# Graph convolutions in blocks of 49 tiles instead of 56, with 25 gathered and 24 picked tiles in each

## The reference, cut to what matters

```python
def rgcn_conv(x, src, dst, edge_type, W, root, bias):      # called twice, W1 and W2
    x_src = x[src]
    for r in range(8):
        msg = msg + jnp.where((edge_type == r)[:, None], x_src @ W[r], 0)
    agg = segment_sum(msg * norm[:, None], dst, ...)
    return agg + x @ root + bias

def _nnconv(x, src, dst, edge_attr, ew, eb, rw, rb):       # called three times
    W = (edge_attr @ ew + eb).reshape(E, 16, 16)
    msg = jnp.einsum('ei,eio->eo', x[src], W)
    agg = segment_sum(msg, dst, ...)
    return agg + x @ rw + rb
```

## Time and profile before

| | |
|---|---|
| three runs, median (lowest to highest) | 14911.91 us (14904.42 to 14941.55) |
| the profiled execution | 14959.53 us, its span 14958.3 us |
| DVE, POOL, PE, ACT busy over the span | 75%, 62%, 55%, 32% |
| the five convolution passes together | some 6.1 ms of the span |

### The profile page before, as it was taken

How to read it: one execution, slowest core, us unless ns; L and a number is a source line. 1 busy time by engine, 2 the same in 40 slices (tenths; PEclk the granted TensorE clock), 3 DMA queues, 4 the chain that set the end, 5 groups by cost and what they waited for, 6 DMA issues and landing times. The chain is left out here.

```text
span 14958.3 us, 147756 instructions
## 1 busy us (share of the span) xinstructions
PE 8297.6 (55%) x41291; PEld 5702.8 (38%) x41291; DVE 11150.7 (75%) x19230; ACT 4791.5 (32%) x2765; POOL 9259.2 (62%) x6976
## 2 busy tenths in 40 slices
PE   1222222222220688588836566665668858885886
PEld 0111111111110566466623233333356646663664
DVE  6999999999998566466635455554559967995996
ACT  0111111111110466456621001010037746773774
POOL 6777777777752466556655555555337756774776
PEclk5555555555555899789967777787779989997998
DMA  2444444444441222122211111111123323332332
GB/s 83 156 154 153 153 153 156 157 154 153 153 157 40 84 63 67 53 61 67 65 42 36 37 37 34 38 36 37 27 69 114 111 79 100 113 111 67 114 111 73
DMA packets 629773, 1371.10 MB, mean 92 GB/s; under 512 B 262833, under 2 KB 403118, under 8 KB 554126
## 3 DMA queue, kind: packets, MB, share of 16 engines
q1 hardware_dynamic: 405534, 1076.25, 20.0%
q0 software_dynamic: 224112, 293.30, 8.8%
HBM read 656.16 MB, written 712.80 MB: 92 GB/s over the span
## 5 line engine op out<-in xcount | busy, mean ns | idle before, releaser
L536 POOL DMA_INDIRECT h<-in_x,idx x1568 | 3051.7, 1946 | 1206.2 <-DMA efT<-in_edge_attr_t 785.3
L550 PE MATMUL PS<-waug,efT 17*128 17x256 f32 x6272 | 1129.4, 679 | 3167.2 <-DVE e L587 2179.1
L1681 PE MATMUL PS<-hot,lhs 128*128 128x392 bf16 x9408 | 1855.5, 355 | 1228.4 <-issue 762.8
L1668 POOL DMA_INDIRECT myg<-node_table,mix x1568 | 1662.6, 1060 | 1323.1 <-DVE mmsg L1737 797.5
L550 PEld LDWEIGHTS PS<-waug,efT 17*128 17x128 f32 x6272 | 695.2, 313 | 3600.9 <-DVE e L587 2225.8
L1681 PEld LDWEIGHTS PS<-hot,lhs 128*128 128x128 bf16 x9408 | 954.6, 103 | 2129.6 <-issue 1111.2
L1305 PE MATMUL PS<-every_weight,dstf 112*128 112x144 f32 (+1 forms) x8960 | 1313.8, 291 | 493.9 <-DVE dstf L1405 409.0
L1305 PEld LDWEIGHTS PS<-every_weight,dstf 112*128 112x128 f32 x8960 | 1252.3, 197 | 666.4 <-DVE dstf L1405 466.6
L1752 DVE TENSOR_TENSOR lhs<-mkx,m 128x512 bf16<-128x512 bf16 x1176 | 429.5, 421 | 1439.2 <-remote 1092.3
L571 ACT ACTIVATE cf<-cf 128x256 f32<-128x256 f32 x196 | 81.7, 417 | 3843.9 <-DVE e L614 3843.9
L1283 POOL DMA_INDIRECT c0yg<-node_table,c0ix x672 | 859.0, 1278 | 591.7 <-DMA c0ix<-in_src 288.3
(11 more groups left out here) (393 smaller groups left out, 18785.4 us busy)
## 6 DMA issues: line engine op xcount, KB each, us to landing
softmax_maxima<-M SPq DMA_DIRECT2D x196, 1024.0 KB, 8.6
softmax_denominators<-ST SPq DMA_DIRECT2D x196, 1024.0 KB
softmax_numerators<-ST SPq DMA_DIRECT2D x196, 1024.0 KB
r0rb<-pick_b SPq DMA_DIRECT2D x56, 512.0 KB
r0ra<-pick_a SPq DMA_DIRECT2D x56, 512.0 KB
r1rb<-pick_b SPq DMA_DIRECT2D x56, 512.0 KB
r1ra<-pick_a SPq DMA_DIRECT2D x56, 512.0 KB
c0rb<-pick_b SPq DMA_DIRECT2D x56, 512.0 KB
```

Source lines behind the costliest of these rows:

```text
L536: PO.indirect_dma_start(h[b.k][:, q, :], None, io["x"], bass.IndirectOffsetOnAxis(ap=idx[b.k][:, q:q + 1], axis=0))\
L550: mm = PE.matmul(PS[0:CH, 4 * message + 2 * (n % 2) + r, 0:C2], efT[b.k][row:row + D + 1, n // 2, :], waug[row:row + D + 1, C2 * message:C ...
L1668: PO.indirect_dma_start(yg[b.k][:, q, :], None, table8, bass.IndirectOffsetOnAxis(ap=ix[b.k][:, q:q + 1], axis=0))\
L1681: mm = PE.matmul(PS[:, 6 + k, 0:A7 // 2], lhs[(G * b.k + q) % 2][:, r, part, :], hot[4 * ((G * b.k + q) % 2) + r][:, k * A7 // 2:(k + 1) * ...
```

## The change

The blocks become 49 tiles (`TBC`, `NBC = 49, 32`) with 25 gathered and 24 picked tiles (`NG`, `HG = 25, 6`), for all five passes. Slots by three take the place of slots by two in `hot_`, in the PSUM banks of the picked rows (3, 4, 5) and in `mx`; the two loads of 2048 index columns (`ra`, `rb2`) become three of 1024 columns, each with a semaphore of its own. DVE's list of a block is regrouped: five scalings of five tiles, and 11 halvings instead of 13 for c (5 instead of 6 for r); the final add of r, the carry and the scan stand behind the last group. Cut to its core:

```diff
-TBC, NBC = 56, 28
-NG, HG = 24, 8
+TBC, NBC = 49, 32
+NG, HG = 25, 6
...
-            NSC, NTR = (6, 13) if both else (0, 6)
+            NSC, NTR = (5, 11) if both else (0, 5)
...
-            hot_ = [sb(f"{name}hot{k}", [128, KT, 512], F32R, L) for k in TWO]
-            ra = [sb(f"{name}ra{k}", [128, 2048], I16, L) for k in TWO]
-            rb2 = [sb(f"{name}rb{k}", [128, 2048], I16, L) for k in TWO]
-            mx = [dstf[0:A9 * D, 512 * k:512 * k + 512] for k in TWO]
+            hot_ = [sb(f"{name}hot{k}", [128, KT, 512], F32R, L) for k in range(3)]
+            ra = [sb(f"{name}ra{k}", [128, 1024], I16, L) for k in range(3)]
+            rb2 = [sb(f"{name}rb{k}", [128, 1024], I16, L) for k in range(3)]
+            mx = [dstf[0:A9 * D, 512 * k:512 * k + 512] for k in range(3)]
...
                     if m0 == 0:
                         PE.wait_ge(*h_cv.at(groups(b, q + 1)))
-                        if due(m := groups(b, q - 1)):
+                        if due(m := groups(b, q - 2)):
                             PE.wait_ge(*h_mk.at(m))
                     for m in range(m0, m1):
-                        mm = PE.matmul(PS[0:A9 * D, 4 + q % 2, :], parts[:, m % 2, m // 2, :],
-                                       hot_[q % 2][:, m // 2, :], start=(m == 0), stop=(m == 2 * KT - 1))
+                        mm = PE.matmul(PS[0:A9 * D, 3 + q % 3, :], parts[:, m % 2, m // 2, :],
+                                       hot_[q % 3][:, m // 2, :], start=(m == 0), stop=(m == 2 * KT - 1))
...
                 def widen(b, q):
-                    if due(n := groups(b, q - 1)):
+                    if due(n := groups(b, q - 2)):
                         S.wait_ge(*h_g.at(n))
...
                 def mask(b, q):
-                    if due(n := groups(b, q - 1)):
+                    if due(n := groups(b, q - 2)):
                         V.wait_ge(*h_sel.at(n))
...
                 def scale_gathered(b, n):
-                    ts = slice(4 * n, 4 * n + 4)
+                    ts = slice(5 * n, 5 * n + 5)
...
-                    if b and not both:
-                        add_typed(b, 8)
-                        add_typed(b, 9)
+                    if b:
+                        if not both:
+                            add_typed(b, 6)
+                        carry_in(b)
+                        by_destination(b)
```

More of the change, by code:

```diff
@@ L1165, in program @@
         c_ix, c_co, c_st = pair("c_ix"), pair("c_co"), pair("c_st")
-        h_ra, h_rb = pair("h_ra"), pair("h_rb")
-        c_ix, c_co, c_st, h_ra, h_rb = ([Since(x) for x in two_] for two_ in (c_ix, c_co, c_st, h_ra, h_rb))
+        c_ix, c_co, c_st = ([Since(x) for x in two_] for two_ in (c_ix, c_co, c_st))
+        h_ra, h_rb = ([Since(sem(f"{n}{j}")) for j in range(3)] for n in ("h_ra", "h_rb"))
         c_sc, c_pr, c_al, c_tr, c_msg = (Since(sem(n)) for n in ("c_sc", "c_pr", "c_al", "c_tr", "c_msg"))
@@ L1210, in conv_sync, with rows, load_low, load_high @@
             def conv_sync():
[L1211 to L1215, removed]
+                def rows(b, j, from_):
+                    return from_[some(b, NG + 8 * j, 8), :].rearrange("(a t) c -> a (t c)", a=1).to_broadcast([128, 1024])
+                def load_low(b, j):
+                    if due(n := b.on(-1).count(3 * KT, KT * j + KT)):
                         SP.wait_ge(*h_oh.at(n))
                         SP.nop(nofuse=True)
-                    SP.dma_start(rb2[half][:, :], rows(b, half, pick_b)).then_inc(h_rb[half].sem, 16)
-                def load_high(b, half):
-                    if due(n := groups(b.on(-1), 4 * half + 4)):
+                    SP.dma_start(rb2[j][:, :], rows(b, j, pick_b)).then_inc(h_rb[j].sem, 16)
+                def load_high(b, j):
+                    if due(n := groups(b.on(-1), 2 * j + 2)):
                         SP.wait_ge(*h_mk.at(n))
                         SP.nop(nofuse=True)
-                    SP.dma_start(ra[half][:, :], rows(b, half, pick_a)).then_inc(h_ra[half].sem, 16)
+                    SP.dma_start(ra[j][:, :], rows(b, j, pick_a)).then_inc(h_ra[j].sem, 16)
                 def load_ix(b):
@@ L1246, in first @@
                 def first(b):
-                    for half in TWO:
-                        load_low(b, half)
-                        load_high(b, half)
+                    for j in range(3):
+                        load_low(b, j)
                     for k in TWO:
                         load_ix(b.on(k))
+                    for j in range(3):
+                        load_high(b, j)
+                    for k in TWO:
                         load_co(b.on(k))
-                    for half in TWO:
-                        load_low(b.on(1), half)
-                        load_high(b.on(1), half)
+                    for j in range(3):
+                        load_low(b.on(1), j)
+                        load_high(b.on(1), j)
                 def body(b):
@@ L1330, in widen @@
                 def widen(b, q):
-                    S.wait_ge(*h_oh.at(b.count(4 * KT, KT * (q // 2) + KT)))
-                    if due(n := groups(b, q - 1)):
+                    S.wait_ge(*h_oh.at(b.count(3 * KT, KT * (q // 2) + KT)))
+                    if due(n := groups(b, q - 2)):
                         S.wait_ge(*h_g.at(n))
                     at = 512 * (q % 2)
-                    S.activation(hot_[q % 2][:, :, :], hb[q // 2 % 2][:, :, at:at + 512], ACT.Copy).then_inc(h_cv.sem, 1)
+                    S.activation(hot_[q % 3][:, :, :], hb[(3 * b.k + q // 2) % 2][:, :, at:at + 512], ACT.Copy).then_inc(h_cv.sem, 1)
                 def copy_always(b, q):
@@ L1381, in one_hot @@
                 def one_hot(b, j, c):
-                    if j > 3:
-                        b, j = b.on(1), j - 4
+                    if j > 2:
+                        b, j = b.on(1), j - 3
                     if not b.exists():
@@ L1386, in one_hot @@
                     if c == 0:
-                        if j % 2 == 0:
-                            V.wait_ge(*h_rb[j // 2].at(b.count(16, 16)))
+                        V.wait_ge(*h_rb[j].at(b.count(16, 16)))
                         if due(n := groups(b, 2 * j - 2)):
                             V.wait_ge(*h_cv.at(n))
-                    V.tensor_scalar(hb[j % 2][:, c, :], rb2[j // 2][:, 1024 * (j % 2):1024 * (j % 2) + 1024], pick[:, c:c + 1], None,
-                                    ALU.is_equal).then_inc(h_oh.sem, 1)
+                    V.tensor_scalar(hb[(3 * b.k + j) % 2][:, c, :], rb2[j][:, :], pick[:, c:c + 1], None, ALU.is_equal)\
+                        .then_inc(h_oh.sem, 1)
                 def one_hots(nx, p, n):
```

73 lines of the change are left out of this document (34 added, 39 removed).

## The result

The changed kernel takes **15570.84 us** (15521.41 to 15594.16, 4 runs), the kernel before 14926.48 us beside it: ratio 1.0429, 95% interval 1.0395 to 1.0462. The sign of the forecast was right, its size (15150, up to 15430) was not.

What follows compares the result with a forecast made beforehand. Gathers were taken to end each c block, picks with their stall each r block: +321 for three c passes and -82 for two r passes, +239 on 14912, gave 15150 us, range 14860 to 15430.

Steps and rivals of the forecast that it cites:

- Gathers in c: c passes: 800 gathers at 1.527 us end each block, 1222 us; with start pause and edges 1296 us, +107 each.
- 47 us of start pause: Start of a c pass: POOL's wait stays, since block 0's adds can't begin before its gathers are in; 47 us.
- the scaling 0.81: DVE's scaling of gathered rows in c, grown from 512 to 640 elements: taken at 0.81 us, 17 us more in all.
- The excess by DVE's work: Gathers' time over the shortest scales with all DVE work beside POOL: 294 ns a gather in c, 185 in r.
- rival 2: Only one-hots lengthen gathers: 1.477 us a gather in c, +67 a pass, r -41; 15030 us in all; chance 0.12.
- The third slot at 0: Three slots in `hot_`, PSUM and `mx` let PE and ACT run further ahead; worth nothing behind a wait for gathers.
- Rival 3: PE's late semaphores come into c too, 10.8 us a block: +83 a pass, +250, 15400 us; chance 0.18.
- The r passes: Picks plus stall, 36.4 us a block, end each block against 35.4 of gathers: 1233 us against 1274, -41 each.
- 25.6 forecast for the picks: r passes, per block without stall: six groups of picks at 4.26 us each, 25.6 us.
- with stalls of 20 us a block (45.6): r passes if the stall grew to 20 us a block: some +250 us each; no chance given.
- -73 each: r passes if their stalls were absent: 73 us less each.

Runs made afterwards that it cites:

- e13: The kernel before, unchanged, in a set of runs without stalls: 13493.55 us.
- e14: The changed kernel, unchanged, in a set of runs without stalls: 13985.98 us, ratio 1.0368 to the kernel before.
- e15: Changed kernel; r0 third slot unused, r1 POOL waits between blocks; one-hots (c0), halvings (c1), scalings (c2) cut. No stalls; c passes 1181.7, 1131.8, 1173.7 us.
- e16: Changed kernel; third slot unused in r0 and c0, r1's POOL waits before each block until the last landed: r0 1439.4, r1 1268.3, c0 1265.4 us.
- e7: Changed kernel; r0 POOL waits ahead of gathers 12 and 24, r1 40 nops per wait, DVE work cut in c: c passes 1397, 1389, 1389 us.
- e17: Kernel before, POOL waiting for landing ahead of gather 12 (r), 8 and 16 (c's first two blocks), 14 (third layer), with stalls: 13879.85 us, ratio 0.9336.
- e10: Kernel before, POOL waiting for landing ahead of gather 12 (r), 8 and 16 (c's first two blocks), 14 (third layer), without stalls: 13747.75 us, ratio 1.0195.
- e2: Changed kernel, POOL waiting until the last gather landed ahead of every fourth gather in r0, every eighth in r1: r0 1485.9, r1 1276.8 us.
- e4: Kernel before, POOL waiting until the last gather landed ahead of every fourth gather in r0, every eighth in r1: r0 1287.6, r1 1113.5 us.
- e5: Kernel before, POOL waiting for landing ahead of every eighth gather in r and in c's first two blocks: 14455.02 us, ratio 0.976.
- e6: Changed kernel, POOL waiting for landing ahead of every eighth gather in r and in c's first two blocks: 15098.85 us, ratio 1.0203.
- e8: Kernel before, POOL waiting for landing ahead of every twelfth gather in r0, eleventh in r1, seventh in the third layer's stage: 14148.63 us in one run.
- e3: Changed kernel; r0 issues 4 of 14 picking matmuls a group, r1 multiplies gathered rows by the norm at the step's end: r0 1375.3, r1 1502.4 us.

## Why the prediction was wrong

- **Gathers in c, right.** 1.527 us each forecast, (971.9 + 243.2)/800 = 1.519 measured; 47 us of start pause, 49.4 measured; the scaling 0.81, 0.815 measured; 1222 + 47 + 27 = 1296 us against the window's 1292. By the passes' own ends c lost 84 to 97 us and not 107; without the start stall of both kernels it loses 86 to 94 (e13, e14).
- **The excess by DVE's work, right in size in c, not in kind.** One rate for all instructions gave c's mean (294 ns of excess forecast, 275 measured); r's gathers came to 1.375 us for the 1.418 forecast, 34 us a pass less than the sum had. e15's rates differ nearly twofold. The one-hots were the cheapest neighbours and the `tensor_tensor` with two SBUF inputs the dearest, so rival 2 is out. The Trainium skill ("SBUF — State Buffer", Who interferes with whom) infers that a `tensor_tensor` doesn't hold up descriptor generation. e15's 99 and 60 us go against that inference; the measurement decides.
- **The third slot at 0, right within what the runs tell** (e16: 25 us in r0 between two sets, within 5 in c0; e15: 1114.2 with two slots against e14's 1114.1).
- **Rival 3, wrong**: c's steady blocks have next to no stall at 1.52 us a gather (two waits of 4.6 and 6.0 us in c2), though POOL never pauses. e7 shows how near it was: at 1.42 it comes.
- **The r passes: the step that failed is "with the stall kept at 10.8 a block 36.4 us. That is 1.0 more than the gathers".** I took picks with their stall and gathers as two chains side by side, of which only the longer counts, and POOL as pausing in each block. Measured are some 45 us a block, half of the 89.9 between restarts: 13.5 of stall (8.18 + 18.86 in two blocks), 4.7 of wait for the gathers (9.49 in two) and 26.7 for the rest (25.6 forecast for the picks). So the stall term was 2.7 us too small, and the wait for the gathers, which the sum had at nothing, adds 4.7: the two stand in one run of POOL one behind the other. That POOL runs over two blocks because gathers and picks are so close in length is argued, not shown. The text had the case, "with stalls of 20 us a block (45.6) it would be some +250 each", and gave it no chance of its own. e16 breaks the pairs and gets 1268.3, of which 45 us, in 21 waits, are the pauses themselves. That this is near the 1233 forecast is partly luck: the stall is 5.4 us a block there (173.7/32), half of the 10.8, and DVE still waits 177.1 us for gathers.
- **Without stalls "-73 each" was wrong too.** It compared an r without stalls to one with them. e13 shows that the kernel before gains more by their absence (1275 to 992) and then is bound by its 672 gathers; 800 cost 119 us more.

So without stalls the loss has one plain cause in all five passes: 128 more gathers a pass on the engine that sets the end, 492 us (e14). With stalls it is 644. Most of the 152 us between them I put down to r, where the stalls add 349 us a pass to the changed kernel (1111 to 1460) and 279 to the one before (991 to 1270); that is a difference between sets of runs, and no single run splits the loss so.

## What to carry to other kernels

When an edit moves work onto a POOL that gathers all the time, price each gather with its pause and with what DVE does beside it, and ask how long POOL now runs without a pause, over the ends of blocks too. When an engine waits "remote" for a semaphore of work that the trace shows as done, put one short wait into the other engine's stream and see whether it goes: here such waits in three places gave 7% where there was the stall (e17). And time both kernels again on another occasion before a gain of this kind is kept, for it may be a loss there: the same kernel lost 2% where there was no stall (e10).

## What the runs showed of the hardware that I had not expected

- In four of six sets of runs PE's semaphores come late while POOL issues indirect gathers 1.25 to 1.42 us apart without a pause, up to 41 us in a pass's first block of the changed kernel. Waits of some 8 us end while POOL still issues, and in e7's c passes longer ones too; the last long one of a run ends up to 7 us after POOL stops. DVE stands still meanwhile and the gathers come faster still, 0.94 + 0.30 us, which fits that the last stall lasts to the run's end (argued, not shown). In r held 4 leaves no stall (e2, e4) and held 8 under 25 us a pass (e2, e4 to e6); held 7 leaves none in the third layer (e8), and held 11 to 14 leaves 62 to 171 us a stage (e7, e8, e17).
- The stall cost the kernel before some 1.4 ms of 14.9: 14.80 to 14.99 ms in four sets, 13.49 in two. The number of PE's picking matmuls isn't the cause (e3). What it is in the hardware, and why two sets had none, stays open. POOL's issuing and the landing of what it issues change together in every run here, so which of the two makes PE's semaphores late wasn't told apart either.
- Whether the landing or the time of the pause ends the stall stays open: 40 nops on POOL make no gap between its gathers (e7).
- Less work on DVE can make a pass slower: e7's c passes took 9% more.
